# First tile's adapter product from the joint products, on-chip row copies and another load order in a fused adapter and expert layer

## The reference

```python
# first layer, adapter A, B chosen by adapter_mapping[tile]
y = einsum('bti,oi->bto', x, W) + b
y = y + einsum('btr,bro->bto', einsum('bti,bir->btr', x, lora_As[m]), lora_Bs[m]) * 2.0
# second layer
base = y @ base_w.T + base_b
res_hidden = y @ A.T                      # 64 wide
logits = y @ router_w.T                   # 16 experts
probs = softmax(logits); topw, topi = top_k(probs, 2)
topw = topw / (sum(topw) + 1e-6)
delta = einsum('bse,bsr,eor->bso', combine(topw, topi), res_hidden, B)
out = x + base + delta * 0.5
```

## Time and profile before

| what | us |
|---|---|
| median of 3 runs | 112.12 (111.91 to 113.07) |
| profiled execution | 113.04 |
| its span, first to last instruction | 111.2 |
| PE busy | 99.9 (90%) |
| VectorE busy | 63.4 (57%) |
| ACT busy | 38.8 (35%) |
| POOL busy | 21.1 (19%) |
| mean granted TensorE clock | 0.969 |
| moved by DMA | 18.28 MB, 164 GB/s over the span |

### The profile page before, as it was taken

How to read it: one execution, slowest core, us unless ns; L and a number is a source line. 1 busy time by engine, 2 the same in 40 slices (tenths; PEclk the granted TensorE clock), 3 DMA queues, 4 the chain that set the end, 5 groups by cost and what they waited for, 6 DMA issues and landing times.

```text
span 111.2 us, 1781 instructions
## 1 busy us (share of the span) xinstructions
PE 99.9 (90%) x577; PEld 89.6 (81%) x577; DVE 63.4 (57%) x170; ACT 38.8 (35%) x90; POOL 21.1 (19%) x33
## 2 busy tenths in 40 slices
PE   5997999499902999999999999999999999999990
PEld 5786998399802999999799789879978788888990
DVE  0524995996400706489986647747744948282211
ACT  4316616864320164627362523241052244040000
POOL 3000083000067019900814101800000000000000
PEclk9999999999997559999999999999999999999999
DMA  3999579944999980628738280814500536320211
GB/s 90 237 365 332 168 219 349 420 156 135 268 337 311 206 173 23 178 44 199 271 121 196 40 242 22 228 57 122 150 23 21 184 116 175 108 94 0 94 53 47
DMA packets 8493, 18.28 MB, mean 164 GB/s; under 512 B 1427, under 2 KB 3859, under 8 KB 8228
## 3 DMA queue, kind: packets, MB, share of 16 engines
q1 hardware_dynamic: 6356, 11.06, 36.1%
q10 hardware_dynamic: 2128, 7.11, 18.1%
HBM read 14.34 MB, written 3.38 MB: 159 GB/s over the span
## 4 chain that ended last, share of the span: by engine, by line
PE 74%; DMA 7%; DVE 6%; issue 6%; SPq 3%; ACT 2%
PE pair L706 70%; DMA w_raw_all<-w_cat 7%; DVE bias_part L535 2%; SPq L242 1%; PE pair L822 1%; DVE w_lo_all L541 1%; PE pair L824 1%; ACT w_hi_all L364 1%; PE pair L813 1%; PE pair L833 1%; SPq L238 1%; DVE p_lo L549 1%; ACT bp_hi L398 1%; DVE bp_lo L560 1%; DVE bias_part L531 1%
## 5 line engine op out<-in xcount | busy, mean ns | idle before, releaser
L706 PE MATMUL pair<-e_hi,w_hi_all 128*128 128x512 f32 (+1 forms) x72 | 27.3, 379 | 0.0
L706 PE MATMUL pair<-e_lo,w_hi_all 128*128 128x512 f32 (+1 forms) x72 | 26.5, 369 | 0.0
L706 PE MATMUL pair<-e_hi,w_lo_all 128*128 128x512 f32 (+1 forms) x72 | 26.5, 368 | 0.0
L706 PE MATMUL pair<-p_hi,x_hi 128*128 128x304 f32 x64 | 21.1, 330 | 0.0
L706 PE MATMUL pair<-p_lo,x_hi 128*128 128x304 f32 x64 | 20.4, 318 | 0.0
L706 PE MATMUL pair<-p_hi,x_lo 128*128 128x304 f32 x64 | 20.4, 318 | 0.0
L706 PEld LDWEIGHTS pair<-e_hi,w_hi_all 128*128 128x128 f32 x72 | 13.5, 187 | 2.7
L706 PEld LDWEIGHTS pair<-e_hi,w_lo_all 128*128 128x128 f32 x72 | 13.5, 187 | 2.6
L706 PEld LDWEIGHTS pair<-e_lo,w_hi_all 128*128 128x128 f32 x72 | 13.5, 188 | 1.7
L318 POOL TENSOR_TENSOR x_lo<-xt_raw,x_hi 128x512 fp32r<-128x512 f32 x6 | 7.7, 1282 | 36.7 <-ACT x_hi L370 36.7
L465 ACT ACTIVATE w_hi_all<-exp_raw_all 128x512 fp32r<-128x512 f32 x16 | 9.7, 629 | 13.4 <-DVE exp_raw_all L648 13.4
(11 more groups left out here) (80 smaller groups left out, 135.2 us busy)
## 6 DMA issues: line engine op xcount, KB each, us to landing
w_raw_all<-spill SPq DMA_DIRECT2D x16, 256.0 KB, 3.9
exp_raw_all<-experts ACTq DMA_DIRECT2D x4, 512.0 KB, 7.1
out<-xn SPq DMA_DIRECT2D x7, 256.0 KB, 3.1
w_raw_all<-w_cat SPq DMA_DIRECT2D x3, 552.0 KB, 6.5
c_stack<-c_spill SPq DMA_DIRECT2D x7, 148.0 KB, 8.1
xn<-x_n ACTq DMA_DIRECT2D x2, 512.0 KB, 9.7
xt_raw<-x_t ACTq DMA_DIRECT2D x1, 1024.0 KB, 7.5
xn<-x_n ACTq DMA_DIRECT2D x1, 1024.0 KB, 7.3
```

Source lines behind the costliest of these rows:

```text
L706: return nc.tensor.matmul(out_ap, lhs, rhs, start=first, stop=last)
```

## The change

- c products of all tiles come right behind the fold; `FOLDS` is (1, 0, 2, 3), so that the bank they use is free first. The bias matmuls move behind the first tile's transpose; on ACT bp_hi comes behind split_experts(1), on VectorE bias_part and bp_lo between the low parts of the fold.
- The first tile's h is put unsplit in columns 0 to 15 of a zeroed 128 x 128 tile (`h_first`), transposed, split into high and low, and multiplied with all of c_hi and c_lo (the rows of the other tiles meet zeros), 6 matmuls; two more with ones (K = 2) add the bias rows. So tile 0 reads no copied rows.
- Tiles 1 to 7 have their rows of c_stack written by SP from c_hi and c_lo on chip, two DMAs a tile, each row doubled (32 rows a DMA). The row order is h_hi, h_lo in pairs a, r, b. The DRAM tensor c_spill, its two writes and seven reads go.
- The bias rows are made by one VectorE instruction in c_stack of tile 1 (row 64 the high part, row 65 the rest) and copied to tiles 2 to 7 by one DMA.
- Load order: experts 0 and 1 before the wait for xt; xt 4 to 7 and xn 2, 3 before the fold's splits on ACT, behind lb_hi; xn 4 to 7 on SP behind the first spread_routing. x_lo of tiles 0 and 1 and lb_lo move ahead of the bias steps on VectorE; POOL's a-parts wait for ph_done.
- In the first tiles, routing_transpose(0) comes ahead of lora_product(1), x_hi(3) ahead of split_experts(3), split_experts_lo(1) behind route(0).

```diff
-FOLDS = (2, 1, 0, 3)
+FOLDS = (1, 0, 2, 3)
# SP
-            for n, (part, done) in enumerate(((bias_hi, bh_done), (bias_lo, bl_done))):
-                sp.wait_ge(done, 1)
-                sp.dma_start(c_stack[HR + n:HR + n + 1, :, :].bitcast(F32),
-                             part[0:1, :].unsqueeze(1).to_broadcast([1, NT, W2N]).bitcast(F32)
-                             ).then_inc(stacked_bias, 16)
-            for part, done, rows in ((c_hi, ch_done, 0), (c_lo, cl_done, 2)):
-                sp.wait_ge(done, 1)
-                for n in range(rows, rows + 2):
-                    sp.dma_start(c_stack[n:HR:4, 0, :].bitcast(F32),
-                                 part[0:R, :].bitcast(F32)).then_inc(stacked[0], 16)
-            sp.wait_ge(c_spilled, 32)
-            for t in range(1, NT):
-                sp.dma_start(c_stack[0:HR, t, :].bitcast(F32),
-                             c_spill[t].rearrange("r m n -> (r m) n")).then_inc(stacked[t], 16)
+            def stack_rows(t):
+                for part, done, row in ((c_hi, ch_done, 0), (c_lo, cl_done, 2 * R)):
+                    sp.wait_ge(done, 1)
+                    sp.dma_start(c_stack[row:row + 2 * R, t, :].bitcast(F32),
+                                 part[R * t:R * t + R, :].unsqueeze(1).to_broadcast([R, 2, W2N]).bitcast(F32)
+                                 ).then_inc(stacked[t], 16)
+            for t in range(1, 5):
+                stack_rows(t)
+            sp.wait_ge(bias_rows, 1)
+            sp.dma_start(c_stack[HR:HT, 2:NT, :].bitcast(F32),
+                         c_stack[HR:HT, 1:2, :].to_broadcast([2, NT - 2, W2N]).bitcast(F32)
+                         ).then_inc(stacked_bias, 16)
+            for t in range(5, NT):
+                stack_rows(t)
-            for t in range(NB):
+            spread_routing(0)
+            sp.dma_start(xn[:, 4:NT, :], x_n[:, 4:NT, :]).then_inc(in_xn[2], 16)
+            for t in range(1, NB):
                 spread_routing(t)
# GpSimd
+            pool.memset(h_first[:, :], 0.0).then_inc(consts, 1)
+            pool.wait_ge(ph_done, 1)
             lora_a_parts(0)
# ScalarE
+            load_experts(0)
+            load_experts(1)
             act.wait_ge(in_xt[0], 16)
             x_hi_part(0)
             x_hi_part(1)
-            load_experts(0)
-            load_experts(1)
             act.dma_start(xt_raw[:, 2:4, :], x_t[:, 2:4, :]).then_inc(in_xt[1], 16)
             load_experts(2)
-            act.dma_start(xn[:, 0:2, :], x_n[:, 0:2, :]).then_inc(in_xn[0], 16)
-            load_experts(3)
-            act.wait_ge(bias_step, KC + 1)
-            nc.scalar.activation(bp_hi[:, :], bias_part[:, :], ACT.Copy).then_inc(bph_done, 1)
-            folded_hi(0)
             act.wait_ge(in_lora, 16 * NT)
...
-            for n in range(1, KC):
+            act.dma_start(xn[:, 0:2, :], x_n[:, 0:2, :]).then_inc(in_xn[0], 16)
+            load_experts(3)
+            act.dma_start(xt_raw[:, 4:NT, :], x_t[:, 4:NT, :]).then_inc(in_xt[2], 16)
+            act.dma_start(xn[:, 2:4, :], x_n[:, 2:4, :]).then_inc(in_xn[1], 16)
+            for n in range(KC):
                 folded_hi(n)
-            act.wait_ge(pe_bias, 1)
-            nc.scalar.activation(bias_hi[:, :], w2_cols(ps_b)[0:1, :], ACT.Copy).then_inc(bh_done, 1)
             act.wait_ge(pe_warm, 1)
             split_experts(0)
             split_experts(1)
+            act.wait_ge(bias_step, KC + 1)
+            nc.scalar.activation(bp_hi[:, :], bias_part[:, :], ACT.Copy).then_inc(bph_done, 1)
             act.wait_ge(pe_c, 1)
             nc.scalar.activation(c_hi[:, :], w2_cols(ps_c), ACT.Copy).then_inc(ch_done, 1)
-            for n, (part, done) in enumerate(((c_hi, ch_done), (c_lo, cl_done))):
-                act.wait_ge(done, 1)
-                act.dma_start(c_spill[:, :, 2 * n:2 * n + 2, :].rearrange("t r a n -> (t r) a n"),
-                              part[:, :].unsqueeze(1).to_broadcast([P, 2, W2N]).bitcast(F32)
-                              ).then_inc(c_spilled, 16)
...
-            lora_hi(0)
+            lora_first()
             split_experts(2)
+            lora_first_t()
             act.wait_ge(in_xt[1], 16)
-            lora_t(0)
-            act.dma_start(xt_raw[:, 4:NT, :], x_t[:, 4:NT, :]).then_inc(in_xt[2], 16)
-            act.dma_start(xn[:, 2:4, :], x_n[:, 2:4, :]).then_inc(in_xn[1], 16)
             x_hi_part(2)
+            act.wait_ge(pe_bias, 1)
+            nc.scalar.activation(bias_hi[HR:HT, :], w2_cols(ps_b)[HR:HT, :], ACT.Copy).then_inc(bh_done, 1)
             lora_hi(1)
             exps(0)
             lora_t(1)
# VectorE
+            x_lo_early(0)
+            x_lo_early(1)
             dve.wait_ge(lbh_done, 1)
...
+            bias_part_of(0)
+            bias_part_of(1)
+            folded_lo(0)
+            folded_lo(1)
+            bias_part_of(2)
+            folded_lo(2)
+            folded_lo(3)
+            bias_part_of(3)
+            dve.wait_ge(bph_done, 1)
...
+            def stack_bias():
+                dve.wait_ge(bh_done, 1)
+                dve.wait_ge(low_row_set, 2)
+                nc.vector.scalar_tensor_tensor(out=c_stack[HR:HT, 1, :], in0=bias_hi[HR:HT, :].bitcast(F32),
+                                               scalar=low_row[HR:HT, 0:1], in1=w2_cols(ps_b)[HR:HT, :],
+                                               op0=ALU.mult, op1=ALU.add).then_inc(bias_rows, 1)
             split_experts_lo(0)
-            lora_lo(0)
+            lora_first_lo()
+            stack_bias()
+            lora_lo(1)
+            read_z(0)
+            route(0)
             split_experts_lo(1)
-            read_z(0)
-            lora_lo(1)
-            route(0)
+            lora_lo(2)
             read_z(1)
# TensorE
+            def lora_first_product():
+                border = BANK - z_small[0]
+                def part(lhs, rhs, last):
+                    nc.tensor.matmul(ps_z[0][:, z_small[0]:BANK], lhs, rhs[:, 0:border],
+                                     start=False, stop=last, skip_group_check=True)
+                    return nc.tensor.matmul(ps_z[0][:, BANK:BANK + W2N - border], lhs, rhs[:, border:],
+                                            start=False, stop=last, skip_group_check=True)
+                pe.wait_ge(ht_done, 1)
+                pe.wait_ge(ch_done, 1)
+                part(ht_first_hi[:, :], c_hi, False)
+                pe.wait_ge(cl_done, 1)
+                part(ht_first_hi[:, :], c_lo, False)
+                pe.wait_ge(ht_first_done, 1)
+                part(ht_first_lo[:, :], c_hi, False)
+                pe.wait_ge(bias_rows, 1)
+                part(ones[HR:HT, :], c_stack[HR:HT, 1, :], True).then_inc(pe_z, 1)
...
             x_first(0)
             x_other(0)
-            lora_transpose(0)
+            lora_first_transpose()
+            bias()
             x_first(1)
-            lora_product(0)
+            lora_first_product()
             x_other(1)
             lora_transpose(1)
             x_first(2)
+            routing_transpose(0)
             lora_product(1)
-            routing_transpose(0)
             x_other(2)
```

More of the change, by code:

```diff
@@ L524, in _, with x_lo_early @@
                                     ALU.subtract).then_inc(wl_done, 1)
+            for k in range(1, KC):
+                dve.wait_ge(wh_done, k + 1)
+                nc.vector.tensor_tensor(w_lo[:, k, :], w_raw[:, k, :], w_hi[:, k, :].bitcast(F32),
+                                        ALU.subtract).then_inc(wl_done, 1)
+            def x_lo_early(t):
+                dve.wait_ge(xh_done, t + 1)
+                nc.vector.tensor_tensor(x_lo[:, t].rearrange("p k n -> p (k n)"), xt_raw[:, t, :],
+                                        x_hi[:, t].rearrange("p k n -> p (k n)").bitcast(F32),
+                                        ALU.subtract).then_inc(xl_early, 1)
             def bias_part_of(k):
@@ L537, in bias_part_of @@
                                                    op0=ALU.mult, op1=ALU.add).then_inc(bias_step, 1)
-            for k in range(1, KC):
-                dve.wait_ge(wh_done, k + 1)
-                nc.vector.tensor_tensor(w_lo[:, k, :], w_raw[:, k, :], w_hi[:, k, :].bitcast(F32),
-                                        ALU.subtract).then_inc(wl_done, 1)
-            for k in range(KC):
-                bias_part_of(k)
             def folded_lo(n):
@@ L556, in split_experts_lo @@
                                         ALU.subtract).then_inc(el_done, 1)
-            folded_lo(0)
-            dve.wait_ge(bph_done, 1)
-            nc.vector.tensor_tensor(bp_lo[:, :], bias_part[:, :], bp_hi[:, :].bitcast(F32),
-                                    ALU.subtract).then_inc(bpl_done, 1)
-            folded_lo(1)
+            x_lo_early(0)
+            x_lo_early(1)
             dve.wait_ge(lbh_done, 1)
@@ L567, in _ @@
                                     ALU.subtract).then_inc(lbl_done, 1)
-            for n in range(2, KC):
-                folded_lo(n)
-            for t in range(2):
```

(32 more changed lines are left out.)

69 lines of the change are left out of this document (40 added, 29 removed).

## The result

The changed kernel's median is 111.41 us over 20 runs (107.0 to 112.49), against 112.76 for the kernel before over 20. The ratio given with them, 0.9606 (95% interval 0.9531 to 0.9681), sets the fastest executions of each against each other, and of the changed kernel those are only two (107.0 and 107.98). The changed kernel is faster, by 1 to 1.5% in the usual execution and by 4% in its best ones. The forecast was 104.1 with a range up to 107.1, and 111.41 lies outside.

The account below looks back on a forecast made before the run. TensorE was taken as the bound, losing time to holes, a stall and half clock before x_other(2). That starting 8.4 us earlier, less 0.4 wait at the experts, gave 8.0 off and 104.1 us; range 102.9 to 107.1.

Parts of the forecast that it names:

- the landing of the tables: Adapter tables on SP's queue, ahead of lb_hi: taken to land at 15.5 us, bounds 14.4 and 17.
- the stall: TensorE's idle piece of 4.97 us before the first tile's adapter product, reader of c_stack; forecast to go.
- Rival A: Front late through tables at 17 or ACT's issues at 1.43 us each; 105.7 to 107.4 us, chance 0.17.
- D: SP's row issues at 1.46 us; experts wait 10.6 us and the clock falls; 117 us, slower than before, chance 0.04.
- E: Clock stays at 0.50 there even without an idle stretch, 2.7 us more; 106.8 us, chance 0.04.
- B: SP queue bounds tile 0: row issues of 0.75 to 0.9 us, wait 1.5 to 3.4; 105.2 to 107.1, chance 0.18.
- C: Bias rows replace the DRAM round trip: steps behind c_lo 1.5 us later, PE waits 1; 105.1 us, chance 0.07.
- The bias copy: Bias rows to tiles 2 to 7, twelve rows on two DMA engines; up to 2 us, not in the sum.
- ScalarE's four issues: Four DMA issues behind lb_hi, ahead of folded_hi(0): about 0.55 us each, ending near 18.9, hidden behind VectorE.
- The xn load: xn 4 to 7, 1 MB on SP's queue ahead of spill(1): delays it 2.6 us, hidden by a whole iteration.
- The zero-padded product: First tile's lora_first_product: 8 matmuls instead of 2, padding free, six added matmuls cost 0.83 us.
- The rule of the Trainium skill: DMA engines alternate between queues by packet, so the tables would end late, toward products starting at 21.5 us.

Follow-up runs that it names:

- e1: Changed kernel with expert loads 0 and 1 issued behind the two x_hi again, as in the kernel before; 107.14 us, ratio 0.9491 to the kernel before.
- a0: The changed kernel itself, measured again beside other runs; 110.73 us, ratio 0.9868 to the kernel before.
- f1: Changed kernel with only the load of xn 4 to 7 put back on ScalarE's queue; 110.60 us, ratio 0.9856 to the kernel before.
- e7: Changed kernel with 18 filler matmuls of 192 columns ahead of the fold's last block, results not used; 110.64 us, ratio 0.9841 to the kernel before.
- e10: e4 with the three expert loads and xt 2, 3 issued behind lb_hi; 107.64 us, ratio 0.9468 to the kernel before.
- f4: The kernel of e9 measured again in another group; 104.92 us, ratio 0.9373 to the kernel before.
- e4: Changed kernel, expert loads 0 and 1 behind x_hi again and work reordered around the wait for the tables; 104.99 us, second run 106.86.
- e6: Changed kernel, work reordered around the table wait, xn 4 to 7 on ScalarE's queue, row copies of tiles 5 to 7 behind the first spread_routing; 108.4 us.
- e9: e4 with the load of xn 4 to 7 back on ScalarE's queue; 104.48 us, ratio 0.9325 to the kernel before.
- e2: Kernel before with only expert loads 0 and 1 issued ahead of the wait for xt; 113.97 us, ratio 1.0118 to the kernel before.

## Why the prediction was wrong

The sum was worked out for one order of events, and one term of it was wrong: "I take 15.5" for the landing of the tables. Measured: 17.95, 18.46, 19.2, 19.3 us in four profiles with that order on both engines; its upper bound was 17. The room was read off one microsecond at 0.32 busy, and the experts filled it. The prediction's own numbers could have said so: the two expert loads are 1 MB, 2.6 us at its 406 GB/s, and one microsecond at 0.32 has room for some 0.3 MB. Undoing that alone gives 3.6 us (e1).

Step by step, forecast and the profiled execution:

| step | forecast | measured |
|---|---|---|
| tables landed | 15.5 | 17.95 |
| adapter products start | 19.9 | 22.16 |
| clock behind them | 1.00 | 0.50 for 3 us, +1.7 us |
| x_first(0) to x_other(2), own time | as worked out | +0.2 (first product waits 0.19) |
| x_other(2) starts | 33.9 | 38.07 |
| wait at the experts | 0.4 | 0.16 |
| experts start | 43.7 | 47.81 |
| experts to PE's end | 57 | 57.4 |

2.3 + 1.7 + 0.2 makes the 4.2 us. That is the profiled execution, 109.55 us; the median is 1.9 us above it. Two more profiles with this front show where such executions lose more: in a0 (110.35 us) the tables landed at 19.2, the products started at 23.41 and the experts at 48.73; in f1 (112.23 us) the hole was 4.50 us, the clock stood at 0.50 from 23 to 28 us, and the experts started at 50.41. So the mechanism named was right (the stall goes, and behind the adapter products TensorE works through but for 0.19 and 0.16 us), and the sizes of its middle were right to 0.2 us. Rival A named the place and the cause, late tables, and priced them at 105.7 to 107.4; it was short, because it left out two things that hang on the same delay. One is the clock: it was given to D and E alone, and not to A, though a hole of 2 to 4 us stood in A's own sum (0.5 and 1.6 to 3.3 more). The other is SP: the rows were costed from c_hi at 25.1, and A moved TensorE but not c_hi; the row copies began at 27.94, and their end, 37.80, lay 0.6 us under TensorE's path. In the profiled execution this cost nothing; in e7, with the clock's cost gone, the chain goes through it.

B's price was wrong: a row copy took 0.59 to 0.62 us to issue in every profile (median), as the nearest row said, and in the changed kernel's profile SP's queue held nothing back. Its place was right once the front is on time: in e1, e10, f4 and e7 the chain goes through the row copies, and there the landing of the spill behind them (2.1 to 3.7 us, 1.41 in the sum) is what costs. C didn't happen beyond 0.19 us; D and E not at all. The bias copy, set beside the sum at up to 2 us, cost nothing: it was issued at 33.18 in 0.76 us, and no matmul waited for it. One bound was added up wrong: with products at 19.4 and no wait at the experts the terms give 103.2, not 103.0; nothing hangs on it.

Two edits were called hidden. ScalarE's four issues took 2.5 us (17.96 to 20.47), one of them 1.18, where 2.2 were forecast; folded_hi(0), forecast to end near 18.9, came at 20.52, nearly all of it by the late tables. VectorE was still at the bias steps until 21.33, so in the changed kernel they were hidden, as said; in e10 the same issues were not. The xn load "a whole iteration" ahead of its use was costed at 2.6 us for the spill behind it; spill to broadcasts took 7.1 us in e4's second run, and the load was worth up to 2.4 us, hidden in the changed kernel by the late front.

The zero-padded product cost what was forecast: pieces of 0.13 to 0.14 us each, in the chain of the changed kernel:

```profile
33.04 0.14 PE pair L846
33.18 0.13 PE pair L844
```

The rule of the Trainium skill that had been set beside the sum (DMA: Bandwidth & Descriptors, section on queues, rings and completion order: each DMA engine takes turns between queues) pointed to late tables, and the traces agree: 14.0 and 14.8 us with nothing on the other queue, 17.95 and later with the experts ahead in all profiles but one (e6, by 16.8), and 0.02 instead of 0.09 MB of SP's queue in the microsecond from 13 us.

The time forecast, 104.1, is about what the kernel of e9 and f4 reaches (104.48 and 104.92), with the same first-tile product, row copies and bias rows, and three parts of the load and work order turned round. It is faster than both kernels.

## What to carry to other kernels

A transfer that runs in a gap of the DMA engines takes its share from what is still on its way (here 0.09 MB of the tables' queue in one microsecond became 0.02), and the price is paid by what stands behind the late one: before a load is pulled ahead, list everything queued behind each transfer it will meet, and price the delay through all of it (the engine's wait, the clock after the hole, and every queue that starts from the same result). Keep what the bottleneck needs ahead of the wait for a transfer. Think twice before a large load goes into the queue that carries small, urgent ones: with 1 MB ahead of it, a spill of 8 KB had its broadcasts 6.0 and 7.1 us behind it, without it 2.9 us. Whether that costs anything depends on whether the bottleneck waits for it (nothing to 2.4 us here). And run the best kernel more than once: one kernel's median moved by 1.9 us between two groups (e4), as much as the effect that was looked for.

## What the runs showed of the hardware

- The granted clock fell to 0.50 after holes of 2.87 us (the changed kernel) to 4.50 us (f1), but also after 1.5 and 0.35 us in e2, and not after 1.9 us in e1 and e7. It falls in some executions of one kernel and not in others (mean clock 0.966 to 1.0 over six runs of the changed kernel).
- Tables issued at the same times (the last at 12.1 to 12.9 us) landed between 14.0 and 20.9 us: 14.0 and 14.8 with no load on ScalarE's queue beside them, 14.4 to 16.7 in the three profiles where something waited for them and the experts were issued from 12.2 to 13.2 us, 17.95 to 20.9 with the experts issued from 10.2 to 11.8, but for one (e6), where they were there by 16.8.
- Matmuls with K = 128 of mostly zeros, with K = 66 and with K = 2 took the same 0.13 to 0.14 us for some 296 columns.
- A spill of 8 KB landed in 1.4 to 1.8 us, but in 2.1 to 3.7 when it was issued at most 0.11 us behind the row copies, and once in 2.6 with 0.6 us between.
- Copies between partitions on chip, 32 rows of 2,368 bytes, took 0.59 to 0.62 us to issue (median) in all profiles, whatever ran beside them. They landed in 2.4 to 2.6 us in the changed kernel, and in up to 6.0 in e4 and e9, where they went out 4 to 5 us earlier.
